# Slot layer of a decoder block: alpha in one tile, output product on 64 rows, slot inputs copied unscaled and divided in the gates' sums

## The reference

```python
h = gelu(ctx @ w1.T + b1)                       # ctx = [LN(x), mean slot]
route_logits = (h @ w2.T + b2) / (abs(tau) + 0.1)
topk_vals, topk_idx = top_k(route_logits, 8)
alpha = softmax weights of the 8, 0 elsewhere   # (tokens, slots)
slot_input = einsum('bts,btd->bsd', alpha, x)   # x here is LN(x)
slot_wsum = alpha.sum(axis=1) + 1e-08
gi = slot_input / slot_wsum[..., None]
gx = gi @ gru_wih.T + gru_bih ; gh = hs @ gru_whh.T + gru_bhh
r, z = sigmoid(xr + hr), sigmoid(xz + hz)
n = tanh(xn + r * hn)
h_new = (1 - z) * n + z * hs
slot_values = h_new @ wv.T + bv
out = einsum('bts,bsd->btd', alpha, slot_values) @ wo.T + bo
```

## Time and profile before

| | us |
|---|---|
| three runs | 1475.72, 1472.70, 1472.42; median 1472.7 |
| the profiled execution | 1474.58 |
| its span, first to last instruction | 1472.8 (1.8 lie around it) |
| slot stage, first statistics to last y | 1199.8 to 1470.2 of the span |
| TensorE busy in the span | 1406.9 (96%) |
| VectorE, ScalarE, GpSimd busy | 1092.7 (74%), 899.9 (61%), 813.5 (55%) |

### The profile page before, as it was taken

The page is one execution under the profiler, slowest core; times in us unless marked ns, Lnnn a source line. Parts: engine busy times, 40 slices in busy tenths (PEclk is TensorE's granted clock), DMA queues, the critical chain, the costliest instruction groups (busy, mean ns, idle before and its releaser), DMA issues. The chain is left out here.

```text
span 1472.8 us, 57209 instructions
## 1 busy us (share of the span) xinstructions
PE 1406.9 (96%) x22238; PEld 1064.6 (72%) x22238; DVE 1092.7 (74%) x3032; ACT 899.9 (61%) x1573; POOL 813.5 (55%) x1145
## 2 busy tenths in 40 slices
PE   6999999999999999996999999999999959999997
PEld 4777777777777777774777777777777736766774
DVE  6777777777777777764477777877777768999986
ACT  2555555555555655553667676666767537778874
POOL 3455445554455544553377787777777743433442
PEclk9999999999999999998999999999999979999999
DMA  5500000000000000000300000000000000100111
GB/s 164 158 2 1 0 0 0 0 0 0 0 0 0 0 0 0 1 2 14 113 17 15 21 14 21 14 21 14 21 15 14 3 1 16 37 33 31 36 36 43
DMA packets 31207, 32.40 MB, mean 22 GB/s; under 512 B 3937, under 2 KB 29602, under 8 KB 31138
## 3 DMA queue, kind: packets, MB, share of 16 engines
q1 hardware_dynamic: 31138, 31.46, 6.9%
HBM read 23.06 MB, written 8.39 MB: 21 GB/s over the span
## 5 line engine op out<-in xcount | busy, mean ns | idle before, releaser
L1077 POOL TENSOR_SCALAR_AFFINE_SELECT a_probs_t<-a_probs_t 128x512 f32<-128x512 f32 x256 | 161.9, 666 | 62.6 <-ACT a_probs_t L709 62.6
L1613 DVE TENSOR_REDUCE c_neg_max<-score_banks 128x8 f32<-128x512 f32 (+1 forms) x128 | 116.6, 952 | 82.7 <-PE score_banks L1346 82.7
L1778 POOL TENSOR_SCALAR_AFFINE_SELECT c_probs_t<-c_probs_t 128x512 f32<-128x512 f32 x256 | 153.3, 634 | 14.9 <-ACT c_probs_t L1540 14.4
L1091 POOL TENSOR_TENSOR a_less<-a_attn,a_remote 128x512 f32<-128x512 f32 x31 | 39.5, 1274 | 214.3 <-DVE a_attn L884 214.3
L709 ACT ACTIVATE a_probs_t<-score_banks 128x2048 f32<-128x2048 f32 x64 | 120.2, 1878 | 47.4 <-PE score_banks L554 47.4
L1540 ACT ACTIVATE c_probs_t<-score_banks 128x2048 f32<-128x2048 f32 x64 | 120.2, 1878 | 26.4 <-PE score_banks L1374 26.4
L397 PE MATMUL side_banks<-a_xn_t,a_w_qk 128*128 128x256 f32 x512 | 134.2, 397 | 1.6 <-ACT a_xn_t L654 0.7
L861 DVE TENSOR_REDUCE a_neg_max<-score_banks 128x8 f32<-128x512 f32 (+1 forms) x128 | 116.4, 951 | 5.9 <-PE score_banks L524 5.9
L397 PEld LDWEIGHTS side_banks<-a_xn_t,a_w_qk 128*128 128x128 f32 x512 | 92.9, 196 | 12.9 <-issue 2.3
L2206 POOL TENSOR_TENSOR r_hn<-rz_t,half_hn 128x256 f32<-128x256 f32 x32 | 23.3, 729 | 138.9 <-ACT rz_t L2034 138.9
L664 ACT ACTIVATE a_k_z<-side_banks,a_b_k,row_half 128x256 f32<-128x256 f32 x128 | 61.7, 562 | 53.8 <-PE side_banks L397 53.8
(11 more groups left out here) (271 smaller groups left out, 3898.5 us busy)
## 6 DMA issues: line engine op xcount, KB each, us to landing
x_sb<-in_x SPq DMA_DIRECT2D x32, 256.0 KB, 2.9
ctx_in<-in_ctx SPq DMA_DIRECT2D x32, 256.0 KB, 2.7
out<-y SPq DMA_DIRECT2D x32, 256.0 KB, 2.1
w_ih<-in_ffn_w_ih SPq DMA_DIRECT2D x1, 768.0 KB, 4.8
w_hh<-in_ffn_w_hh SPq DMA_DIRECT2D x1, 768.0 KB, 6.2
a_raw_qk<-in_attn_qk_w SPq DMA_DIRECT2D x1, 512.0 KB, 3.8
a_raw_cross<-in_xattn_qk_w SPq DMA_DIRECT2D x1, 512.0 KB, 5.0
b_ih<-in_ffn_b_ih SPq DMA_DIRECT2D x1, 384.0 KB, 6.5
```

The source lines that it names most:

```text
L1077: nc.gpsimd.affine_select(out=probs, in_=probs, pattern=[[0, 4], [1, 128]], compare_op=ALU.is_ge, fill=0.0, base=-1, channel_multiplier=-1 ...
L1613: ins = nc.vector.tensor_reduce(neg_max[:, tt, :].rearrange("p (i s l) -> p i s l", i=4, s=2)[:, :, :, late], all_scores[:, :, :, 128 * (1 ...
L1778: nc.gpsimd.affine_select(out=heads, in_=heads, pattern=[[0, 4], [1, 128]], compare_op=ALU.is_ge, fill=0.0, base=0, channel_multiplier=-1) ...
```

## The change

Four edits, all in `slots`.

1. Alpha of both sequences lies in one 128x128 tile: sequence 0 in columns 0 to 63, sequence 1 in columns 64 to 127. One transpose gives both (slots of sequence 0 in rows 0 to 63, of sequence 1 in rows 64 to 127), and ScalarE copies 128 columns where it copied 256. The memset of alpha is gone.
2. The output product takes 64 rows for each sequence, into two different PSUM banks. An increment of a semaphore stands ahead of it on TensorE.
3. The slot inputs are copied from PSUM unscaled by ScalarE, the sum's column with them (`copy_sums`, 257 columns, between `gates` and `copy_xn`). VectorE's scaling of `gi` is gone; `invert_sums` (1e-8 and the reciprocal) reads the copied column and stands behind `candidate`. The division is made later: `rz` and `n_in` become scalar_tensor_tensor instructions that multiply the product from PSUM by `w_inv` and add the constant.
4. PSUM is laid out anew: hidden and logits share a bank, so `hidden` waits for the logits of the pair before; the slot inputs move to the last bank.

```diff
-    alpha_all = sb("alpha", [128, 2, 2, PS])
-    alpha = [alpha_all[:, i, :, :] for i in range(2)]
-    alpha_t = [sb(f"alpha_t{i}", [128, 2, 128]) for i in range(4)]
+    alpha = [sb(f"alpha{i}", [128, PS]) for i in range(2)]
+    alpha_t = [sb(f"alpha_t{i}", [PS, 128]) for i in range(4)]
...
             def hidden(at):
                 pe.wait_ge(xnT_ready, at.count(1, 1))
                 wait(pe, hid_ready, at.count(1, 0))
+                wait(pe, logit_ready, at.count(1, 0))
...
-                for tt in range(2):
-                    mm = pe.transpose(out_bank[:, 128 * tt:128 * tt + 128], alpha[at.par][:, tt, :], ident[:])
-                mm.then_inc(alphaT_filled, 1)
+                pe.transpose(alphaT_bank[:, 0:128], alpha[at.par][:], ident[:]).then_inc(alphaT_filled, 1)
...
             def transpose_inputs(at):
-                pe.wait_ge(in_step, at.count(3, 3))
+                pe.wait_ge(in_copied, at.count(1, 1))
...
-                for tt in range(2):
-                    mm = pe.matmul(out_bank[:, D * tt:D * tt + D], alpha_t[at.off % BY][:, tt, :], slot_val[:],
+                pe.sem_inc(cross.pe_turn, 1)
+                for tt in range(2):
+                    half = slice(SLOTS * tt, SLOTS * tt + SLOTS)
+                    mm = pe.matmul(out_banks[:, tt, :], alpha_t[at.off % BY][half, :], slot_val[half, :],
                                    start=True, stop=True, skip_group_check=True)
...
+            def copy_sums(at):
+                act.wait_ge(in_filled, at.count(1, 1))
+                wait(act, giT_filled, at.count(1, 0))
+                wait(act, in_step, at.count(2, 0))
+                nc.scalar.activation(gi[:], in_bank[:, 0:XW], ACT.Copy).then_inc(in_copied, 1)
...
-                for back, what in ((3, gates), (0, copy_xn), (4, copy_slots), (2, copy_alpha),
+                for back, what in ((3, gates), (2, copy_sums), (0, copy_xn), (4, copy_slots), (2, copy_alpha),
                                    (2, copy_inputs), (3, candidate), (1, exp), (0, gelu)):
...
-            def mean_inputs(at):
-                dve.wait_ge(in_filled, at.count(1, 1))
-                nc.vector.tensor_scalar(w_sum[:], in_bank[:, D:XW], 1e-8, None, ALU.add).then_inc(in_step, 1)
-                dve.wait_ge(in_step, at.count(3, 1))
-                nc.vector.reciprocal(w_inv[:], w_sum[:]).then_inc(in_step, 1)
-                dve.wait_ge(in_step, at.count(3, 2))
-                wait(dve, giT_filled, at.count(1, 0))
-                nc.vector.tensor_scalar(gi[:], in_bank[:, 0:D], w_inv[:, 0:1], None, ALU.mult).then_inc(in_step, 1)
+            def invert_sums(at):
+                dve.wait_ge(in_copied, at.count(1, 1))
+                nc.vector.tensor_scalar(w_sum[:], gi[:, D:XW], 1e-8, None, ALU.add).then_inc(in_step, 1)
+                dve.wait_ge(in_step, at.count(2, 1))
+                nc.vector.reciprocal(w_inv[:, at.par:at.par + 1], w_sum[:]).then_inc(in_step, 1)
...
-                nc.vector.tensor_tensor(rz[:], gate_bank[0][:], rz_const[:], ALU.add).then_inc(rz_ready, 1)
+                dve.wait_ge(in_step, at.count(2, 2))
+                nc.vector.scalar_tensor_tensor(rz[:], gate_bank[0][:], w_inv[:, at.par:at.par + 1], rz_const[:], ALU.mult,
+                                               ALU.add).then_inc(rz_ready, 1)
...
-                nc.vector.tensor_tensor(n_in[:], gate_bank[1][:, 0:D], r_hn_c[:], ALU.add).then_inc(n_in_ready, 1)
+                nc.vector.scalar_tensor_tensor(n_in[:], gate_bank[1][:, 0:D], w_inv[:, at.par:at.par + 1], r_hn_c[:], ALU.mult,
+                                               ALU.add).then_inc(n_in_ready, 1)
...
-                if fed.real:
-                    mean_inputs(fed)
...
                 if updated.real:
                     candidate(updated)
+                if fed.real:
+                    invert_sums(fed)
...
-            nc.vector.memset(alpha_all[:], 0.0).then_inc(set_up, 1)
```

More of the change, by code:

```diff
@@ L106, in decoder @@
             with ExitStack() as scope:
-                slots(nc, scope, sem, a, out, bank, x_sb, ident, cross, slot_weights)
+                slots(nc, scope, sem, a, out, score_banks, bank, x_sb, ident, cross, slot_weights)
 class SlotWeights:
@@ L1812, in _, with slots @@
             pairs(pool, step, TAIL, ahead=1)
-def slots(nc, scope, sem, a, out, bank, x_sb, ident, cross, w):
+def slots(nc, scope, sem, a, out, score_banks, bank, x_sb, ident, cross, w):
     def sb(name, shape, dt=F32):
@@ L1843, in slots @@
     chosen_inv = sb("chosen_inv", [128, 2])
[L1844 to L1846 removed]
+    alpha = [sb(f"alpha{i}", [128, PS]) for i in range(2)]
+    alpha_t = [sb(f"alpha_t{i}", [PS, 128]) for i in range(4)]
     w_sum = sb("w_sum", [128, 1])
[L1848 to L1849 removed]
+    w_inv = sb("w_inv", [128, 2])
+    gi = sb("gi", [128, XW])
     gi_t = sb("gi_t", [128, C, PS])
@@ L1864, in slots @@
     set_up, dve_turn = sem("f_set_up"), sem("f_dve_turn")
-    tr_bank, hid_bank, logit_bank, in_bank, gate_bank, new_bank, out_bank = (
-        bank[0], bank[1], bank[2], bank[3], bank[4:6], bank[6], bank[7])
+    tr_bank, hid_bank, logit_bank, in_bank, gate_bank, new_bank = (
+        bank[0], bank[1][:, 0:PT], bank[1][:, PT:PT + 2 * SLOTS], bank[7], bank[4:6], bank[6])
+    alphaT_bank, out_banks = bank[2], score_banks[:, 2:4, 0:D]
     def s(name):
@@ L1909, in slot_inputs @@
                     half = slice(SLOTS * tt, SLOTS * tt + SLOTS)
-                    mm = pe.matmul(in_bank[half, 0:XW], alpha[at.par][:, tt, half], xn[at.off % BY][:, tt, :],
+                    mm = pe.matmul(in_bank[half, 0:XW], alpha[at.par][:, half], xn[at.off % BY][:, tt, :],
                                    start=True, stop=True, skip_group_check=True)
@@ L1933, in hidden @@
                 wait(pe, hid_ready, at.count(1, 0))
+                wait(pe, logit_ready, at.count(1, 0))
                 for c in range(C):
-                    mm = pe.matmul(hid_bank[:, 0:PT], w.w1[:, c, :], xn_t[:, c, :], start=(c == 0), stop=(c == C - 1))
+                    mm = pe.matmul(hid_bank, w.w1[:, c, :], xn_t[:, c, :], start=(c == 0), stop=(c == C - 1))
                 mm.then_inc(hid_filled, 1)
@@ L2006, in gelu @@
                 wait(act, logit_filled, at.count(1, 0))
-                nc.scalar.activation(h_t[:], hid_bank[:, 0:PT], ACT.Gelu, bias=b1_all[:, 0:1]).then_inc(hid_ready, 1)
+                nc.scalar.activation(h_t[:], hid_bank, ACT.Gelu, bias=b1_all[:, 0:1]).then_inc(hid_ready, 1)
             def copy_alpha(at):
@@ L2011, in copy_alpha @@
                 wait(act, out_filled, at.count(1, 1 - BY))
-                nc.scalar.activation(alpha_t[at.off % BY][:].rearrange("p t n -> p (t n)"), out_bank[:, 0:256],
-                                     ACT.Copy).then_inc(alphaT_ready, 1)
+                nc.scalar.activation(alpha_t[at.off % BY][:], alphaT_bank[:, 0:128], ACT.Copy).then_inc(alphaT_ready, 1)
             def copy_inputs(at):
@@ L2088, in route_logits @@
                 wait(dve, exp_ready, at.count(1, 0))
-                nc.vector.scalar_tensor_tensor(logits[:], logit_bank[:, 0:2 * SLOTS].rearrange("p (t n) -> p t n", t=2),
+                nc.vector.scalar_tensor_tensor(logits[:], logit_bank.rearrange("p (t n) -> p t n", t=2),
                                                inv_tau[:, 0:1], w.b2[:].unsqueeze(1).to_broadcast([128, 2, SLOTS]),
@@ L2116, in route_weights @@
                 for tt in range(2):
-                    nc.vector.tensor_scalar(alpha[at.par][:, tt, SLOTS * tt:SLOTS * tt + SLOTS], chosen[:, tt, :],
+                    nc.vector.tensor_scalar(alpha[at.par][:, SLOTS * tt:SLOTS * tt + SLOTS], chosen[:, tt, :],
                                             chosen_inv[:, tt:tt + 1], None, ALU.mult).then_inc(alpha_ready, 1)
```

8 lines of the change are left out of this document (3 added, 5 removed).

## The result

The changed kernel took 1478.93 us (median of four runs, 1477.83 to 1481.49), the kernel before 1472.56 beside it: a ratio of 1.0039, with a 95% interval of 1.0025 to 1.0054. Repeated on another chip the ratio was 1.0040 (1.0027 to 1.0053). The change is slower by some 0.4%, and 1478.1 was forecast. One of the twelve runs of a later kernel, the division part alone with the inverse early, took 3604.23 us and is left out of its ratio.

The account below looks back on a forecast made before the run. TensorE's 7.74 us loop was taken as the bound, a 7.46 chain through VectorE close behind, growing by 0.43 per pair. Loop pairs +4.3, first six +2.2, ends -1.1 gave +5.4 on 1472.7: 1478.1 us, range 1472 to 1482.

Parts of the forecast that it names:

- Two loops: Slot stage: TensorE's own loop of 7.74 us per pair and a loop through VectorE of 7.46, side by side.
- the chain: `rz`, `rz_t`, `r_hn`, `r_hn_c`, `n_in`, then VectorE's order to the next `rz`: 7.46 us per pair, 0.28 under the bound.
- TensorE's relief counts: Rival: additions behind `n_in` total under 0.10, the 7.56 loop decides, time falls to 1467.0 us; chance 0.10.
- the 0.43 per pair: VectorE's additions: 0.06 each for scalars in `rz` and `n_in`, 0.19 `w_sum` to reciprocal, 0.12 reciprocal to statistics.
- TensorE's gain: Output product on TensorE: 0.96 goes, 0.68 comes with 64-row halves running at once, gaining 0.28 us per pair.
- The turning and the early pair: Pair where the loops turn: 7.76 + 0.43 = 8.19 us; early pair, 7.90 before, takes the whole 0.43.
- the reading of `n_in`'s wait: VectorE's wait ahead of `n_in`, 0.22 us, is for GpSimd's `r_hn_c`; work removed before `n_in` shortens nothing.
- the 21 pairs: Pairs in the slot stage's loop: +0.82 us per four pairs, 0.205 each, +4.3 in all.
- the first six: Slot stage's first pairs: two take the whole 0.43 us, the other four some 0.33, together +2.2.
- The ends: Slot stage's start and end: memset's 0.44, the 0.35 wait for `gi` and smaller terms go, together -1.1 us.
- The Trainium skill on short reads: `w_sum` reading SBUF instead of PSUM: 0.065 us shorter, time 1.8 lower at 1476.3 us; left out of the sum.
- What would show it: Slot-stage signs: `r_hn_c` wait 0.8 us per pair, no `slot_val` wait, TensorE idle 0.4, `n_in` to statistics 0.7.

Follow-up runs that it names:

- the division part alone with the inverse early: Kernel before with the deferred division only, `w_sum` and reciprocal ahead of `n_in`, products still on 128 rows: 1476.32 us, ratio 1.0014.
- TensorE's part and a late `slot_val`: Kernel before with only the alpha and output-product edits, `slot_val`'s addition moved behind `f_xn`'s scaling: 1469.16 us, ratio 0.9956 to the kernel before.
- the second traces: Kernel before and changed kernel each profiled once more, nothing changed: 1474.84 us in one run and 1480.01 us, ratio 1.0040.
- the early inverse: Changed kernel with `w_sum` and the reciprocal moved from behind `n_in` to ahead of it: 1470.95 us, ratio 0.9972 to the kernel before.

## Why the prediction was right, and where it was not

**The mechanism was right.** Two loops run side by side, TensorE's relief becomes a wait for alpha, VectorE's relief becomes waits of its own, and the additions behind `n_in` go on the chain that then decides. The two halves tried apart, and the inverse on either side of `n_in`, show it. The pair was forecast at 7.89 and is 7.88. The rival "TensorE's relief counts" is what happens as soon as the inverse stands elsewhere.

**The terms of the 0.43 per pair.** The scalars cost 0.06 each, as priced. `w_sum` to the reciprocal measured 0.17 (0.19 forecast), the reciprocal to the statistics 0.14 (0.12). The sum is the same.

**TensorE's gain** of 0.28 is 0.24: from the gates' start to the slot inputs' it was 2.58 + 0.96 = 3.54, and with TensorE's part and a late `slot_val` it is 1337.96 - 1334.66 = 3.30. It plays no part in the changed kernel.

**The turning and the early pair failed.** The turning one was forecast at 8.19 and is 8.07, the early one, 7.90 before, at 8.33 and is 7.93. The sum made the 21 pairs +4.3 and they are +3.57 (166.39 - 162.82); the first six +2.2, and they are +1.31. The step that failed is the reading of `n_in`'s wait in these pairs as GpSimd's. `n_in` starts 0.10 after `r_hn_c` ends in a normal pair (1341.19 to 1341.29). In the early pair the releaser had long been done:

```profile
1239.60 0.72 POOL L2209 TENSOR_TENSOR r_hn_c<-r_hn,n_const 128x256 f32<-128x256 f32 x1
```

It ends at 1240.32 and `n_in` starts at 1240.88, 0.56 later; in the turning pair the distance is 0.24. There it was not GpSimd that ended the wait. What did, the rows don't show: VectorE is idle from the end of `top`, its instruction ahead of `n_in`, at 1240.19.

```profile
1239.84 0.35 DVE L2095 MAX8 top<-logits 128x8 f32<-128x64 f32 x2
```

The changed kernel's VectorE comes to `n_in` earlier, and most of this lateness falls into the longer wait; the same early pair:

```profile
1238.26 0.72 POOL L2214 TENSOR_TENSOR r_hn_c<-r_hn,n_const 128x256 f32<-128x256 f32 x1
```

```profile
1239.18 0.48 DVE L2140 SCALAR_TENSOR_TENSOR n_in<-side_banks,w_inv,r_hn_c 128x256 f32<-128x256 f32 x1 [0.78 <-POOL r_hn_c L2214]
```

1238.98 to 1239.18, 0.20 in place of 0.56, pays most of that pair's 0.43. Of `n_in`'s place in the turning pair, 3.36 before and 3.30 after with 0.06 more in `rz`, 0.12 went the same way. So VectorE's shorter work was not worth zero everywhere; it paid in the pairs where `n_in` came later than GpSimd's result let it. Nor are the normal pairs' 0.22 free room: in all of them `n_in` comes 0.22 or 0.23 after the end of `top`, and with the early inverse 0.19 is still left between `top` and `w_sum`, which waits for nothing of GpSimd's. VectorE's own order and GpSimd's result came within some 0.05 us of each other.

**The ends.** They were put at -1.1. The start, first statistics to first `rz`, gave -0.70 (22.71 to 22.01), and in the second traces -0.52. The memset's part is in it: the first `f_xn` comes 2.19 after the first statistics where it came 2.68 after them. The clock is in it too: it rose 0.9 us sooner, and in the second traces some 0.5. The last written-out pairs gave +0.16, not less. The tail gave +1.50 between the first traces, where the kernel before had its last products at the upper level, and -0.65 between the second ones (12.20 to 11.55), where both had them at the lower one. With the second traces the slot stage is 276.55 - 272.64 = 3.9 us longer: +4.9 for the pairs, -1.0 for the ends. The forecast had +5.4, the medians say 5.9 (4.0 to 7.8). What the medians show beyond 3.9 is not in the slot stage of these traces, and stays open. So the forecast had the pairs 1.6 us too high and lacked these 2.0, and its total is close by luck; the layers ahead of it end anywhere between 1197.9 and 1202.1 in the traces of this case.

**The Trainium skill on short reads.** `w_sum` measured 144 ns from SBUF in the changed kernel, 154 from SBUF in the one with the early inverse, and 150 ns from PSUM in the one before. The Trainium skill, page "VectorE: DVE Perf Modes", section "The TRN2 errata — SBUF-src ops pay a fixed extra latency per instruction", would have it 65 ns shorter from SBUF, an estimate from that page's cycles; this case's rows don't agree. The prediction was right to leave it out of the sum.

**What would show it** came nearly as written for the normal pairs. The wait ahead of `n_in` is smaller than said: 0.66 a pair and 18.3 us over the 27 that the view lists, where some 0.8 and over 20 were said. Part of VectorE's freed time became another wait, ahead of the logits:

```profile
DVE logits L2092 <- PE score_banks L1918: 7.6, 27, 0.9
```

The rest is as it was said: no wait ahead of `slot_val`, 0.3 of TensorE's idle time behind alpha (0.4 was said), 0.71 from `n_in` to the statistics, 0.70 for the output product.

## What to carry to other kernels

When two loops of nearly one length run side by side, ask of every instruction that a change adds on which side of the wait it stands: here two instructions of 0.15 us behind a wait cost some 8 us, and ahead of it next to nothing, while the relief of the busiest engine paid only once they were out of the way. Before a wait is charged to its releaser, subtract the releaser's end from the waiter's start: what is left beyond the usual 0.10 is not the releaser's, and here most of it went when the waiter had less work ahead of it. A wait may be filled with work, but only as far as the instruction behind it stays on time.
